# Attention on one core: VectorE's register reads of node tiles, moved in its program order

## The reference

```python
def _gat_layer(x, src, dst, W, a_src, a_dst, b, heads, concat):
    h = (x @ W).reshape(n, heads, -1)
    al_s = jnp.einsum('nhf,hf->nh', h, a_src)
    al_d = jnp.einsum('nhf,hf->nh', h, a_dst)
    e = jax.nn.leaky_relu(al_s[src] + al_d[dst], NEG_SLOPE)
    m = jax.lax.stop_gradient(jax.ops.segment_max(e, dst, num_segments=n))
    ex = jnp.exp(e - m[dst])
    denom = jax.ops.segment_sum(ex, dst, num_segments=n)
    alpha = ex / (denom[dst] + 1e-16)
    out = jax.ops.segment_sum(h[src] * alpha[:, :, None], dst, num_segments=n)
    ...
```

## Time and profile before

| what | value |
|---|---|
| median of 3 runs | 7596.78 us |
| lowest and highest | 7591.75, 7597.13 us |
| the profiled execution | 7631.7 us, span of its instructions 7629.9 us |
| mean granted TensorE clock | 0.775 of full speed |
| VectorE busy | 4221.6 us, 55% |
| TensorE busy (matmuls) | 5056.5 us, 66% |
| ScalarE busy | 3052.0 us, 40% |
| PoolE busy | 3630.5 us, 48% |

### The profile page before, as it was taken

How to read it: one execution, slowest core, us unless ns; L and a number is a source line. 1 busy time by engine, 2 the same in 40 slices (tenths; PEclk the granted TensorE clock), 3 DMA queues, 4 the chain that set the end, 5 groups by cost and what they waited for, 6 DMA issues and landing times. The chain is left out here.

```text
span 7629.9 us, 101786 instructions
## 1 busy us (share of the span) xinstructions
PE 5056.5 (66%) x22722; PEld 3666.1 (48%) x22850; DVE 4221.6 (55%) x12411; ACT 3052.0 (40%) x8036; POOL 3630.5 (48%) x3680
## 2 busy tenths in 40 slices
PE   5666699995666666666666667566666666666662
PEld 4454588883444444444444445344444444444442
DVE  8999676664444444444444458344444444444446
ACT  6774222222545455455454545223333232323231
POOL 2433211113555555555555534555555555555551
PEclk8778899997777777777777779677777776767776
DMA  8999544332333333333333325233333333333336
GB/s 332 377 388 385 211 128 135 108 113 75 89 90 89 90 88 90 89 90 90 90 89 90 89 67 143 80 84 83 83 82 83 83 82 84 82 84 83 84 83 218
DMA packets 366311, 953.85 MB, mean 125 GB/s; under 512 B 101650, under 2 KB 193734, under 8 KB 340950
## 3 DMA queue, kind: packets, MB, share of 16 engines
q0 software_dynamic: 168928, 459.50, 22.4%
q1 hardware_dynamic: 188470, 440.33, 16.1%
q10 hardware_dynamic: 8640, 51.39, 1.6%
HBM read 686.06 MB, written 264.87 MB: 125 GB/s over the span
## 5 line engine op out<-in xcount | busy, mean ns | idle before, releaser
L253 POOL DMA_INDIRECT rows<-table_d,idx x3328 | 3164.8, 951 | 2373.3 <-PE pG L314 911.1
L314 PE MATMUL pG<-rows,onehot 128*128 128x264 f32 (+1 forms) x6656 | 2434.0, 516 | 712.9 <-issue 551.5
L542 DVE TENSOR_TENSOR acc<-acc,pG 128x264 f32 (+1 forms) x3328 | 1417.3, 426 | 2240.9 <-remote 872.4
L314 PEld LDWEIGHTS pG<-rows,onehot 128*128 128x128 f32 x6656 | 1648.0, 260 | 1346.1 <-issue 756.2
L406 ACT ACTIVATE rows<-rows 128x64 f32<-128x64 f32 (+1 forms) x4480 | 1280.3, 373 | 158.6 <-issue 158.1
L399 ACT ACTIVATE onehotT<-pQ 128x1024 bf16<-128x1024 f32 (+1 forms) x512 | 442.8, 865 | 2034.8 <-PE pQ L286 1283.7
L388 ACT ACTIVATE onehot<-pQ 128x1024 f32<-128x1024 f32 (+1 forms) x512 | 441.5, 862 | 952.9 <-DMA pre_in<-pre_d 506.4
L967 PE MATMUL pH<-hT_pre,w1h 128*128 128x256 f32 x1568 | 470.1, 465 | 183.5 <-ACT hT_pre L828 148.5
L286 PE MATMUL pQ<-drow,k_nrow 128*128 128x512 bf16 (+1 forms) x768 | 341.4, 508 | 324.9 <-ACT onehot L388 238.9
L967 PEld LDWEIGHTS pH<-hT_pre,w1h 128*128 128x128 f32 x1568 | 365.8, 240 | 272.2 <-ACT hT_pre L828 164.9
L1104 DVE SCALAR_TENSOR_TENSOR run<-run,same_e,ea 128x96 f32<-128x96 f32 x1567 | 492.7, 314 | 5.5 <-DMA ea<-in_ea 4.3
(11 more groups left out here) (297 smaller groups left out, 5318.6 us busy)
## 6 DMA issues: line engine op xcount, KB each, us to landing
rows_d<-run SPq DMA_DIRECT2D x98, 1536.0 KB
ea<-in_ea SPq DMA_DIRECT2D x98, 768.0 KB
rows<-table_d,idx POOLq DMA_INDIRECT x3328
pre_d<-pre ACTq DMA_DIRECT2D x49, 1024.0 KB
pre_in<-pre_d SPq DMA_DIRECT2D x49, 1024.0 KB, 5.1
hrow_c<-table_d SPq DMA_DIRECT2D x98, 256.0 KB
tab<-tab_d SPq DMA_DIRECT2D x64, 260.0 KB
table_d<-g_rows SPq DMA_DIRECT2D x49, 260.0 KB
```

What stands on the lines that cost most here:

```text
L253: g.indirect_dma_start(out=rows[:, at.par, k, 0:XF + H], out_offset=None, in_=table, in_offset=bass.IndirectOffsetOnAxis(ap=idx[:, at.par, ...
L314: mm = pe.matmul(pG[(k + 2 * at.par) % 4][:, 0:W], onehot[:, k, :], rows[:, at.par, k, :], start=True, stop=True)
L542: v.tensor_tensor(to, to, pG[(k + 2 * at.par) % 4][:, 0:W], ALU.add).then_inc(added, 1)
```

## The change

VectorE's read of the 12 early tile numbers of batch `n`, with the wait for its input and the increment of `v_passed`, moves from behind items 20 to 25 to ahead of `scores(n)`, behind items 12 and 13. In the last step but one (`ahead=False`) the 14 late tile numbers of the last batch are read there, too, and kept in `last_late`; the last step (`chain=False`) takes them from there and reads nothing at its start. In all other steps the late read stays at the start. No instruction is added or dropped.

```diff
             def step(b, first=False, chain=True, ahead=True, after=True):
                 n = b.plus(1)
-                if not first:
+                if not chain:
+                    late = last_late[0]
+                elif not first:
                     late = node_tiles(nc, v, jrow_v, b, EARLY, TB)
 
                 def sums(ks):
@@ -556,6 +558,11 @@
                     return
                 destination_sums(n)
                 sums(range(EARLY, 14))
+                v.wait_ge(jv_in[n.par], n.fills * 16 + 16)
+                v.sem_inc(v_passed, 1)
+                early = node_tiles(nc, v, jrow_v, n, 0, EARLY)
+                if not ahead:
+                    last_late.append(node_tiles(nc, v, jrow_v, n, EARLY, TB))
                 scores(n)
                 sums(range(14, 16))
                 local_maxima(n)
@@ -564,9 +571,6 @@
                 sums(range(18, 20))
                 maxima(n)
                 sums(range(20, TB))
-                v.wait_ge(jv_in[n.par], n.fills * 16 + 16)
-                v.sem_inc(v_passed, 1)
-                early = node_tiles(nc, v, jrow_v, n, 0, EARLY)
                 weight(n)
                 weigh(n, 0)
                 rescale(n, early[0])
@@ -594,6 +598,7 @@
             v.sem_inc(max_copied, 1)
             v.sem_inc(weighed_dve, DG)
             v.sem_inc(added, 4)
+            last_late = []
             over_batches(v, s, step)
             v.wait_ge(added, NB * TB + 4)
```

## The result

The changed kernel takes 7644.46 us (median of 5 runs, 7630.13 to 7645.93) where the kernel before takes 7593.73 (5 runs beside it, 7576.93 to 7597.13): +51 us, ratio 1.0061 [1.005, 1.0072]. The forecast was 7731, +134 us. The sign is right and the size is not: less than half of it came. The time lies in the whole range (7580 to 7850) only because that was drawn down for rival (b); the range of the forecast's own mechanism, 7675 to 7850, misses it.

The account below looks back on a forecast made before the run. The prediction took a cycle through the engines as the bound, with VectorE, TensorE and ScalarE all behind `z`. Stage 1 111, plus stage 2 56, minus 33 at L517 gave +134 us: 7731, range 7580 to 7850.

Parts of the forecast that it names:

- (b): Rival: the late aggregated count behind items 14 and 15 hides the read in both stages; faster, 7564 us; chance 0.14.
- the forecast's own mechanism: The read ahead of the scores delays `z`, with little won at L517: +134 us, 7675 to 7850; chance 0.68.
- The price of a read, part 1, stage 1: Read ahead of the scores, four heads: 3.48 us per pair of batches, taken up by no wait behind `z`; 111 us.
- Part 1, stage 2: Read ahead of the scores, one head: half hidden by the wait ahead of items 14 and 15; 56 us, bounds 0 and 111.
- Part 2, L517: Read gone ahead of L517: TensorE lets odd batches win at most 0.84 us (stage 1), 0.18 (stage 2); 33 us gained.
- the forecast's bad bound: From L364 to item 0: TensorE could be slowed as in the 6.80 us case, 44 us lost in stage 1.
- The step that failed: Behind `z` in stage 1: items 14 and 15 follow without gap, later waits are for TensorE work started after `z`; 111 us.
- (a): Rival: the read only moves along one chain, L517 gives back what `z` loses; 0 us, 7597; chance 0.12.
- (c): Rival: code fetch at VectorE's loop-end branch; a shift of the code makes 102 us come or go; chance 0.06.
- (d): Rival: the read would wait for its input at the new place; within 0.2%, its chance put into (a).

Follow-up runs that it names:

- e14: The changed kernel with the pause of e13 added: 8132.16 us, 1.0705 of the kernel before.
- e13: Kernel before, with PoolE's gather of item 16 waiting until VectorE's carries of the batch are done: 7976.87 us, 1.0505 of the kernel before.
- e3: Kernel before with gathers fetching 8 of 128 rows from the third batch on: 6267.06 us, 0.9746 of the kernel before.
- e4: Changed kernel with gathers fetching 8 of 128 rows from the third batch on: 6427.87 us, 0.9997 of the kernel before.
- e8: Kernel before with VectorE's tile numbers laid out 32 words to a batch instead of 26: 7422.14 us, 0.999 of the kernel before.
- e17: Kernel before with VectorE's and TensorE's tile numbers both 32 words wide, as e11, on a chip without late counts: 6322.46 us, 0.9832 of the kernel before.
- e11: Kernel before with VectorE's and TensorE's tile numbers both 32 words wide, on the 7430 us chip: 7418.08 us, 0.9983 of the kernel before.
- e5: Kernel before, unedited, on a chip where it takes about 6432 us: 6433.59 us, ratio 1.0013.

## Why the prediction was right in sign and wrong in size

**The mechanism** held in its first half: the reads moved whole from L517 to L465 at the forecast price, and VectorE's time ahead of `z` is on the cycle. What lies behind `z` was wrong.

**The price of a read, part 1, stage 1**: 3.48 us for a pair forecast, 3.59 and 3.16 measured on the two kinds of chip. Right.

**Part 1, stage 2.** "Half hidden" was a guess between 0 and 111 from one gap in two batches. On the first chip 3.02 of 3.48 us come at `z`. The cover that it named, the wait ahead of items 14 and 15, took up 1.06 us of a pair where 1.74 were forecast, and 2.40 in e14 against e13. Where the counts are in time nearly all of the read is hidden already ahead of `z` (0.47 us of a pair is left), by the wait for gathered rows ahead of L465, which the forecast didn't have. Without this wait (e3 to e4) stage 2 costs 126 us.

**Part 2, L517.** The cap of 0.84 us in odd batches came from one batch. Without late counts it is 1.05 in stage 1 and 0.94 in stage 2 (0.18 forecast); even batches give nothing, as forecast. On the first chip the way from L364 to item 0 got longer by 0.45 to 0.93 us in three of four kinds, nearer to the forecast's bad bound than to its 33 us of gain.

**The step that failed** is the sentence that no wait behind `z` takes the read up in stage 1. It looked at VectorE's adds of items 14 and 15, and took every later wait, being for work that TensorE starts after `z`, to move with `z` by the full length. The wait that did take it up stands later and on another engine, ScalarE's first mask. The waits of ScalarE in the trace of before had it, 157.8 us in 45 waits for the first mask in stage 1 behind a DMA that ended long before; I hadn't asked for them. With what `z` to L364 gave back as a term, 3.48 us of a pair, the sum for stage 1 is 3.59 + 1.24 - 3.48 = 1.35 us for a pair, 42 us for the 31.5 pairs between first and last `z`, against 45 in the traces; for stage 2 3.02 + 0.52 - 3.78 = -0.24, -8 against -5. These sums restate the table and don't test it. The test is e14 over e13, where the term is taken away: stage 1 then costs 126 us instead of 45. For stage 2 the term of 3.78 us is not all the mask's, as said above, and what makes up the rest is open.

**The rivals.** (b) described the shape, a late count that covers the read; at the place that it named, items 14 and 15, this happened in stage 2 and in part, and it didn't win. (a) is out: L517 comes sooner behind L364, but item 0 doesn't on the first chip. (c) is out: the branch in stage 1 stalls for 3.47 us before and 3.46 after at the median, in stage 2 for 0.22 in both. (d) is out: all of the gap ahead of L465 is issue, none of it a wait for a load.

That the two kinds of chip agree on 50 us is a coincidence of different sums: on the one the time behind `z` pays back 3.5 and 3.8 us of a pair, on the other stage 2's reads lie in the wait for the gathers and the way from L364 to item 0 gives back 1.0.

**Open:** what makes TensorE's counts late in the runs on some chips and not on others, and by what path a run of gathers holds them up. That the run matters is shown by e13, as far as one pause can show it. The six gathers are only counted, and on the chip with 7430 us the count tells less (in e8 19 masks late of 53). Open too is what the counts have to do with TensorE's own standing still in e13.

## What to carry to other kernels

Before an instruction is moved ahead of a point that several engines wait for, list the waits of *every* engine behind this point, one instruction of the batch at a time and not by source line, those with an impossible releaser above all: a count that comes late is slack, which a later start can use up. And look at how long a register read is and where its words lie before deciding where to put it: aligning the table (e17, 1.7% where the chip lets it) did more than any place for the read.

## What the runs showed of the hardware

- A register read of 12 words takes 859 ns from a 16-byte boundary and 2737 ns from 8 bytes behind one; of 26 words on TensorE 2.1 and 6.2 us. Moving the table to a boundary took the long ones to 0.86 and 2.1 to 2.3 us (e8, e11).
- The same kernel takes about 6430, 7430 or 7594 us on different chips, at granted clocks of TensorE of 0.84, 0.78 and 0.77 in the profiled runs. On the two slower ones counts of TensorE reach ScalarE, VectorE and PoolE 2 to 3 us late while PoolE issues gathers back to back.
- TensorE stands still between single matmuls of `destinations` in e13, 1.93 us in the lines above, with no wait that the profile shows; in e5 the 26 take 3.04 us without such a gap.
- SyncE's register operations are slow at times on those chips: the MOVE at L208 takes 0.03 us in every batch of e5's stage 1, and over 0.5 us in 26 of 60 of before (longest 0.73).
- A gather of 128 rows holds PoolE for 0.95 us and the next starts 0.30 us later (before, e17); with 8 rows it holds it for 0.86 us (e3, e4).
